# Cross attention and FFN, two layers: the product with V in two pairs of groups instead of four single groups

## What is computed

```python
# block 1: attention with a band, then a crossing of neighbouring sequences
scores = einsum(q, k) / sqrt(8)            # 8 heads of 8 channels
scores = where(abs(i - j) <= 64, scores, lowest)
o = softmax(scores) @ v                    # then out projection, relu, * ctx, w_ct
# block 2: out = x @ weight * scale, scaled down by its norm (tanh and clip)
# block 3: attention over all positions, q and k rotated, k and v from ctx
# block 4: x @ dequantised w_up + LoRA, relu, @ dequantised w_down + LoRA
```

## Time and profile before

| | us |
|---|---|
| median of 3 runs | 1336.01 (1335.77 to 1337.31) |
| profiled execution, its own time | 1332.8 |
| its span | 1331.0 |
| PE busy, share of the span | 1259.3, 95% |
| DVE busy | 906.8, 68% |
| ACT busy | 848.2, 64% |
| POOL busy | 676.3, 51% |

### The profile page before, as it was taken

How to read it: one execution, slowest core, us unless ns; L and a number is a source line. 1 busy time by engine, 2 the same in 40 slices (tenths; PEclk the granted TensorE clock), 3 DMA queues, 4 the chain that set the end, 5 groups by cost and what they waited for, 6 DMA issues and landing times.

```text
span 1331.0 us, 35488 instructions
## 1 busy us (share of the span) xinstructions
PE 1259.3 (95%) x11100; PEld 836.7 (63%) x11100; DVE 906.8 (68%) x1924; ACT 848.2 (64%) x1849; POOL 676.3 (51%) x1169
## 2 busy tenths in 40 slices
PE   6999999999999998768899999999999989999998
PEld 3667676767766765544565656666666546666665
DVE  6878878887888873659999988888888842111110
ACT  2566777767777775556888888888888853222111
POOL 4577788787878765055455445555555211000000
PEclk9999999999999998988999999999999999999999
DMA  8554555445544430033444444444454400000000
GB/s 208 121 135 106 117 119 117 103 117 116 116 113 112 102 85 6 13 80 89 93 105 94 96 95 103 112 103 101 103 113 99 85 2 16 16 16 16 16 16 32
DMA packets 90486, 113.34 MB, mean 85 GB/s; under 512 B 13971, under 2 KB 80275, under 8 KB 82739
## 3 DMA queue, kind: packets, MB, share of 16 engines
q1 hardware_dynamic: 89216, 111.25, 36.3%
q10 hardware_dynamic: 1206, 1.29, 0.3%
HBM read 18.66 MB, written 4.19 MB: 17 GB/s over the span
## 4 chain that ended last, share of the span: by engine, by line
PE 72%; DVE 9%; POOL 6%; issue 4%; ACT 3%; DMA 3%; SPq 1%; POOLq 0%; ACTq 0%; DVEq 0%
PE bank L477 13%; PE bank L437 12%; PE bank L453 11%; PE bank L699 8%; PE bank L690 8%; PE bank L435 5%; DVE row_max L1131 5%; POOL probs L1355 4%; PE bank L489 4%; PE bank L541 2%; PE bank L508 2%; DMA Ks<-Ks 1%; PE bank L648 1%; PE bank L518 1%; PE bank L529 1%
## 5 line engine op out<-in xcount | busy, mean ns | idle before, releaser
L1131 DVE TENSOR_REDUCE row_max<-bank 128x2 f32<-128x384 f32 (+1 forms) x1024 | 597.7, 616 | 110.5 <-PE bank L437 106.2
L735 ACT ACTIVATE probs<-bank 128x384 f32<-128x384 f32 (+1 forms) x1024 | 536.8, 542 | 162.2 <-PE bank L453 151.5
L437 PE MATMUL bank<-Ks,Qs 96*128 96x192 bf16 (+1 forms) x2048 | 372.1, 263 | 15.1 <-DVE row_max L1131 8.8
L453 PE MATMUL bank<-Qs,Ks 128*128 128x192 bf16 (+1 forms) x2048 | 365.6, 260 | 13.5 <-ACT probs L735 12.4
L1355 POOL TENSOR_SCALAR_AFFINE_SELECT probs<-probs 128x256 f32<-128x256 f32 (+1 forms) x512 | 259.3, 530 | 98.7 <-ACT probs L735 78.3
L437 PEld LDWEIGHTS bank<-Ks,Qs 96*128 96x128 bf16 x2048 | 186.7, 99 | 125.8 <-DVE row_max L1131 39.4
L477 PE MATMUL bank<-probs,V 128*32 128x192 f32 (+1 forms) x4096 | 248.3, 360 | 7.2 <-POOL probs L1355 5.9
L453 PEld LDWEIGHTS bank<-Qs,Ks 128*128 128x128 bf16 x2048 | 185.7, 97 | 45.4 <-ACT probs L735 31.7
L435 PE MATMUL bank<-band,ident 128*128 128x384 bf16 x512 | 168.6, 329 | 1.4 <-DMA Ks<-Ks 1.0
L477 PEld LDWEIGHTS bank<-probs,V 128*32 128x32 f32 x4096 | 107.3, 109 | 87.2 <-issue 43.8
L1292 DVE TENSOR_TENSOR X<-bank,X 128x256 f32 (+1 forms) x32 | 13.6, 424 | 185.6 <-PE bank L699 185.6
(11 more groups left out here) (114 smaller groups left out, 1614.3 us busy)
## 6 DMA issues: line engine op xcount, KB each, us to landing
Ks<-Ks SPq DMA_DIRECT2D x64, 576.0 KB
Qs<-Qs SPq DMA_DIRECT2D x128, 192.0 KB
Qs<-Qp SPq DMA_DIRECT2D x192, 64.0 KB
Ks<-Kp SPq DMA_DIRECT2D x192, 64.0 KB
X<-in_x SPq DMA_DIRECT2D x4, 1024.0 KB, 13.4
side<-in_ctx_crossed SPq DMA_DIRECT2D x32, 128.0 KB, 2.1
side<-in_ctx SPq DMA_DIRECT2D x32, 128.0 KB, 2.1
out<-X SPq DMA_DIRECT2D x8, 512.0 KB, 3.0
```

What stands on the lines that cost most here:

```text
L437: last = nc.tensor.matmul(dst[:, blk * win:(blk + 1) * win], Qs[0:SHIFT_ROW, pair[1], h, blk * P:(blk + 1) * P], Ks[0:SHIFT_ROW, pair[1], ...
L453: last = nc.tensor.matmul(dst[:, blk * win:(blk + 1) * win], Ks[:, pair[1], h, blk * P:(blk + 1) * P], Qs[:, pair[1], h, start(blk):start( ...
L735: nc.scalar.activation(probs[:, h % 8, 0:2 * win], exp_bank[h % 2][:, 0:2 * win], ACT.Exp, scale=SCALE).then_inc(s["exped"], 1)
L1131: nc.vector.tensor_reduce(row_max[:, pair[1], h // HEADS, 0, h % HEADS * 2:h % HEADS * 2 + 2], bank_of(pair, h)[:, 0:2 * win].rearrange("p ...
```

## The change

The groups of the product with V are issued two at a time: at head 3 groups 2 and 3 of the pair before, at head 11 groups 0 and 1 of the pair (heads 2 and 10 in layer 1). `probs` gets 12 slots instead of 8, `q_rest` and `k_rest` get one buffer each instead of three, and their writers wait for the split of the pair before. The tiles of the middle stage move to slots 8 to 11 and to `heads_sb`, with one more wait on ACT and an earlier one on DVE.

```diff
--- before.py
+++ after.py
@@ -24,6 +24,7 @@
 OUTSIDE = -1.0e30
 WIN = T // 2 + BAND
 RING = 3
+PROBS = 12
 FFN_BLOCKS = 8
 VALUES_AT = (3, 2)
 X_CHUNKS = 4
@@ -124,14 +125,14 @@
 
         Qs = sb("Qs", [P, RING, HPP, T], bf16)
         Ks = sb("Ks", [P, RING, HPP, T], bf16)
-        probs = sb("probs", [P, 8, 2 * T])
+        probs = sb("probs", [P, PROBS, 2 * T])
         V = sb("V", [P, RING, 2 * 4 * V_STEP])
         xn = sb("xn", [P, RING, T])
         side = sb("side", [P, RING, T])
         Qp = sb("Qp", [P, RING, PARTS, T], bf16)
         Kp = sb("Kp", [P, RING, PARTS, T], bf16)
-        q_rest = sb("q_rest", [P, RING, T])
-        k_rest = sb("k_rest", [P, RING, T])
+        q_rest = sb("q_rest", [P, T])
+        k_rest = sb("k_rest", [P, T])
         rot = sb("rot", [P, 4, T])
         row_max = sb("row_max", [P, RING, 2, PARTS, HPP])
         max_rows = sb("max_rows", [PARTS * HPP, 2, P], bf16)
@@ -145,9 +146,9 @@
 
         ff = sb("ff", [P, PAIRS, T])
 
-        ff0_xT = [probs[:, n // 2, n % 2 * T:(n % 2 + 1) * T] for n in range(FF0_RING)]
-        ff0_xn = [probs[:, 2 + n // 2, n % 2 * T:(n % 2 + 1) * T] for n in range(FF0_RING)]
-        junk = probs[:, 4, :].rearrange("p (a t) -> p a t", a=2)
+        ff0_xT = [probs[:, PROBS - 4 + n // 2, n % 2 * T:(n % 2 + 1) * T] for n in range(FF0_RING)]
+        ff0_xn = [probs[:, PROBS - 2 + n // 2, n % 2 * T:(n % 2 + 1) * T] for n in range(FF0_RING)]
+        junk = heads_sb[:, :].rearrange("p (a t) -> p a t", a=2)
         xT = (Ks[:, 0:2, :, :].rearrange("p a h t -> p (a h t)").bitcast(fp32)[:, 0:4 * T * 2]
               .rearrange("p (a b t) -> p a b t", a=2, b=2))
         ffn_raw = ff[:, 0:PAIRS // 2, :].rearrange("p (n k) t -> p n (k t)", k=2).bitcast(i32)
@@ -156,7 +157,7 @@
         lora_in = lora[:, 0:T + FF]
         lora_out = lora[:, T + FF:2 * (T + FF)]
         hidden = [Qs[:, 0:2, :, :].rearrange("p a h t -> p (a h t)").bitcast(fp32)
-                  .rearrange("p (h t) -> p h t", h=FF // P), probs]
+                  .rearrange("p (h t) -> p h t", h=FF // P), probs[:, 0:FF // P, :]]
 
         bank = [stack.enter_context(nc.psum_tensor(f"bank{n}", [P, 512], fp32)) for n in range(8)]
         exp_bank, pv_bank = bank[2:4], bank[4]
@@ -238,6 +239,10 @@
 
             return part.bitcast(bf16)[:, 1::2]
 
+        def slot_of(pair, h):
+
+            return (HPP * pair[1] + h) % PROBS
+
         def bank_of(pair, h):
 
             return score_bank[(HPP * pair[1] + h) % SCORE_BANKS]
@@ -476,10 +481,15 @@
                         column = (blk * 4 + g) * V_STEP + 32 * j - (g % 2) * (HD + 1)
                         last = nc.tensor.matmul(dst[32 * j:32 * j + 32, first:first + win],
                                                 V[:, pair[1], column:column + 32],
-                                                probs[:, head % 8, blk * win:(blk + 1) * win],
+                                                probs[:, slot_of(pair, head), blk * win:(blk + 1) * win],
                                                 start=(g % 2 == 0 and blk == 0), stop=(g % 2 == 1 and blk == 1),
                                                 skip_group_check=True)
                 last.then_inc(s["pv_done"], 1)
+
+            def values_half(pair, half):
+
+                for g in (2 * half, 2 * half + 1):
+                    values_group(pair, g)
 
             def project(b, name, pair, weight, source, wait):
                 if not active(pair):
@@ -553,7 +563,7 @@
                                                normed[:, pair[1], blk, :, :].rearrange("p a c -> p (a c)"), ident[:, :])
                 last.then_inc(s["B_filled"], 1)
 
-            tail = {0: lambda: values_group(TAIL, 3), 2: lambda: turn_heads(TAIL), 4: lambda: turn_back(TAIL),
+            tail = {0: lambda: values_half(TAIL, 1), 2: lambda: turn_heads(TAIL), 4: lambda: turn_back(TAIL),
                     5: lambda: project_out(TAIL)}
             if l == 0:
                 tail[6] = lambda: cross_mix(at(TAIL, -1))
@@ -585,8 +595,8 @@
                         turn_max("A", p1, 0)
                     score_head(p1, h)
                     shifted_head(r, h)
-                    if h % 4 == VALUES_AT[l]:
-                        values_group(m1 if h < 4 else r, (h // 4 - 1) % 4)
+                    if h % HEADS == VALUES_AT[l]:
+                        values_half(m1 if h < HEADS else r, 1 - h // HEADS)
 
             def run(first):
                 iterations(e, iteration, extra and (lambda n: extra(e, n)), last=False, first=first)
@@ -731,8 +741,8 @@
                 n = num(pair) * HPP + h
                 e.wait_ge(s["shifted"], n + 1)
                 if h % 4 == 0:
-                    wait_some(e, s["pv_done"], num(pair) * 4 + h // 4 - 1)
-                nc.scalar.activation(probs[:, h % 8, 0:2 * win], exp_bank[h % 2][:, 0:2 * win], ACT.Exp,
+                    wait_some(e, s["pv_done"], num(pair) * 4 + h // 4 - PROBS // 4 + 1)
+                nc.scalar.activation(probs[:, slot_of(pair, h), 0:2 * win], exp_bank[h % 2][:, 0:2 * win], ACT.Exp,
                                      scale=SCALE).then_inc(s["exped"], 1)
 
             def high_part(bk, name, pair, parts, column):
@@ -749,7 +759,7 @@
                 else:
                     e.wait_ge(s["rot_sum"], num(pair) * 2 + (1 if name == "q" else 2))
                     rest = q_rest if name == "q" else k_rest
-                    nc.scalar.activation(parts[:, u, 0, :], rest[:, u, :],
+                    nc.scalar.activation(parts[:, u, 0, :], rest[:, :],
                                          ACT.Copy).then_inc(s[f"{name}_high"], 1)
 
             def turn_rows(bk, name, pair, n, column):
@@ -936,6 +946,8 @@
             def between(n):
                 if n in tail:
                     tail[n]()
+                if n == FF0_LAG[1]:
+                    wait_job(e, L[0], 0, "A", "heads", TAIL, "filled")
                 if n == 8:
                     root(0, 0, FIRST_CHUNK)
                 if n == 10:
@@ -1137,8 +1149,8 @@
                 if not active(pair):
                     return
                 e.wait_ge(s[f"{name}_high"], num(pair) + 1)
-                wait_some(e, s[f"{name}_parts"], num(pair) - RING + 1)
-                nc.vector.scalar_tensor_tensor(out=rest[:, pair[1], :], in0=job_bank[bk][:, 0:T],
+                wait_some(e, s[f"{name}_parts"], num(pair))
+                nc.vector.scalar_tensor_tensor(out=rest[:, :], in0=job_bank[bk][:, 0:T],
                                                scalar=b[:, column:column + 1], in1=parts[:, pair[1], 0, :],
                                                op0=ALU.add, op1=ALU.subtract).then_inc(s[f"{bk}_read"], 1)
 
@@ -1274,7 +1286,7 @@
                     iteration(*early(-2)[:1])
 
             e.wait_ge(ffn_ready, PREP_BLOCKS)
-            e.wait_ge(L[0]["pv_done"], PAIRS * 4 - 1)
+            e.wait_ge(L[0]["pv_done"], PAIRS * 4 - 2)
             ff0_steps(ff0, between)
             e.wait_ge(f_keep, PAIRS)
             run(-1, loop_from=4)
@@ -1319,14 +1331,14 @@
                 else:
 
                     e.wait_ge(s[f"{name}_high"], num(pair) + 1)
-                    nc.gpsimd.tensor_tensor(rest[:, u, :], rest[:, u, :], parts[:, u, 0, :],
+                    nc.gpsimd.tensor_tensor(rest[:, :], rest[:, :], parts[:, u, 0, :],
                                             ALU.subtract).then_inc(s[mid], 1)
                     wait_apart(e, (s[mid], num(pair) * 2 + 1))
                     n, total = num(pair), 2
-                nc.gpsimd.tensor_scalar(parts[:, u, 1, :], rest[:, u, :], 1.0, None,
+                nc.gpsimd.tensor_scalar(parts[:, u, 1, :], rest[:, :], 1.0, None,
                                         ALU.mult).then_inc(s[mid], 1)
                 e.wait_ge(s[mid], (n + 1) * total)
-                nc.gpsimd.tensor_tensor(parts[:, u, 2, :], rest[:, u, :], parts[:, u, 1, :],
+                nc.gpsimd.tensor_tensor(parts[:, u, 2, :], rest[:, :], parts[:, u, 1, :],
                                         ALU.subtract).then_inc(s[done], 1)
 
             def rot_sum(bk, name, pair, n, rest):
@@ -1338,8 +1350,8 @@
                                         ALU.mult).then_inc(s["rot_mul"], 1)
                 wait_job(e, s, l, bk, name, pair, "read")
                 e.wait_ge(s["rot_mul"], num(pair) * 2 + n + 1)
-                wait_some(e, s[f"{name}_parts"], num(pair) - RING + 1)
-                nc.gpsimd.tensor_tensor(rest[:, pair[1], :], rot[:, 2 * n, :], rot[:, 2 * n + 1, :],
+                wait_some(e, s[f"{name}_parts"], num(pair))
+                nc.gpsimd.tensor_tensor(rest[:, :], rot[:, 2 * n, :], rot[:, 2 * n + 1, :],
                                         ALU.add).then_inc(s["rot_sum"], 1)
 
             def mask_group(pair, g):
@@ -1347,7 +1359,7 @@
                 if not active(pair):
                     return
                 wait_apart(e, (s["exped"], num(pair) * HPP + 4 * g + 4))
-                first = (g % 2) * 4
```

(1 more changed line is left out.)

## The result

| | before | after |
|---|---|---|
| median | 1335.89 us (1335.19 to 1337.31, 4 runs) | 1360.71 us (1359.1 to 1362.4, 4 runs) |
| profiled execution | 1332.8, span 1331.0 | 1361.61, span 1359.8 |
| granted clock, whole span | 0.984 | 0.981 |
| an iteration of layer 0 (pairs 5 to 25) | 15.00 us | 14.96 us |
| an iteration of layer 1 (pairs 11 to 25) | 14.68 us | 15.93 us |

A forecast was written before the change was run, and what follows sets the result against it. TensorE's queue was taken to bound the kernel. Layer 0's -2 us and layer 1's +16.4, +0.7 and +0.7 gave +16: profiled 1332.8 to 1349, median 1352 (chance 0.72), range 1337 to 1367.

The forecast's parts named there:

- Savings: TensorE's entries and groups cheaper in pairs, late mask in layer 0 gone: 0.65 us an iteration in layer 0, 0.48 in layer 1.
- rival (a): All savings come through in both layers, with no new waits: 33 us, 1303; chance 0.05.
- First, the landing: Next pair's shifted head 0 waits for the maxima's transfer: 0.83 us in layer 1, 0.40 in layer 0 (net 0.26).
- Rival (c): At head 0 the maxima's transfer lands 0.24 us sooner, in 2.03: waits 0.59 and 0.16, total 1340; chance 0.05.
- Second, ACT at head 7: Layer 1: shifted head 7 waits 0.52 us for ACT's exponential of head 5; bounds nothing and 0.96.
- Third, DVE's maxima at head 9: Scores of head 9 wait for DVE's maximum of head 6: 0.25 us in layer 0, 0.13 in layer 1.
- Fourth, SP at head 8 in layer 0: One iteration in three, shifted head 8 waits 0.48 us for late-sent maxima, replacing head 9's 0.25; mean 0.33.
- (b): ACT and DVE keep up at heads 7 and 9, only the maxima's landing costs: 1330, faster; chance 0.07.
- (e): TensorE, waiting more, falls more often to its lower clock of 1.2 GHz, costing some 15 us: 1367; chance 0.07.

The follow-up runs named there:

- single_first1: Changed kernel, but layer 1 with groups 2 and 3 together at head 2, group 0 alone at head 6, group 1 alone at head 10: 1343.33 us.
- slots_only: Changed kernel with its 12 slots, single rests and moved tiles, but the four groups one by one at their old heads in both layers: 1336.76 us.
- maxima_early0: Changed kernel, but in layer 0 the next pair's maxima are transposed and copied at head 11, the transpose ahead of the burst: 1415.24 us.
- single_last1: Changed kernel, but layer 1 with group 3 of the pair before at head 2, groups 0 and 1 at head 10, group 2 at head 14: 1353.41 us.
- bank_b_three: Changed kernel; groups 0, 1 at head 12 (layer 1: group 0 at 6), maxima turned in bank B (layer 0), split before q's rest (layer 1): 1326.40 us.

## Why the prediction came out as it did

The sign and the mechanism were right, the size was short by 9 us (16 to 25), inside the range.

**Savings (right).** 0.65 and 0.48 forecast; -0.65 and -0.47 measured. The bursts take 1.44 in layer 0 and 1.86 to 1.87 in layer 1, as worked out, and the late mask at head 15 no longer holds a group. The Trainium skill's rule (TensorEngine Tiling (Array Packing), Key Properties) that a change of the tiling mode drains TensorE agrees with the entries of 0.09 that went; taken alone it gave rival (a), 1303, and the rows of waits have the answer to that.

**First, the landing (right).** Issue to landing is 2.21 to 2.28 in layer 0 (pairs 5 to 25) and 2.27 to 2.32 in layer 1 (pairs 11 to 25), and the matmul starts 0.05 later, or 0.12 in one iteration of three. 0.76 for 0.83 in layer 1, 0.44 for 0.40 in layer 0. Rival (c) needed 2.03, from the Trainium skill's sum (DMA: Bandwidth & Descriptors, Anatomy of one DMA), and falls; the one landing in the trace of before was the better guide. That 0.14 would come back at the transpose of head 3 was too much: 0.07 did.

**Second, ACT at head 7 (right, a size off).** 0.64 for 0.52. ACT kept to my times: from the end of the burst at head 2 (869.53) to its exponential of head 5 (872.53) it is 3.00, forecast 2.99. TensorE was early: it could have started shifted head 7 at 872.34 + 0.22, 3.03 and not 3.12 after the burst, because the projection and the turned heads at head 5 took 0.87 and not 0.95, as they no longer wait.

**Third, DVE's maxima at head 9 (wrong).** The waits of 0.25 in layer 0 and of 0.13 in layer 1 do not exist. In layer 0 DVE's normalisation became up to 0.26 shorter, which is as much as the wait was to be; in layer 1 the waits at heads 7 and 8, 0.9 together, stand ahead of it (that these two are the causes is my reading, no run tests it).

**Fourth, SP at head 8 in layer 0 (mis-sized).** 0.07 on average for the 0.33 of steps three and four. In the one iteration of three the transfer did land last, after 2.96 on average for the estimated 3.1, but the path from SP's issue to shifted head 8 shrank from 3.53 only to 2.86 without the wait, by 0.67 and not 0.9: a wait of 0.22 for the forecast 0.48. Why the path shrank less was not found. With step three in it, layer 0 has 0.26 less than forecast; against that stand 0.11 more in the first step and 0.17 of small ones that I had not counted. So layer 0's -0.04 for a forecast of -0.06 is partly luck.

**The term that was missing.** In layer 1 the turning back at head 8 waits 0.26 for DVE to read bank B, and its transposes take 0.05 more. I had asked who reads each result that TensorE waits for, and not who still reads each bank that it writes. The rows were there: the group at head 6 stood between k's turned rows and L552 as it stood before shifted head 7. single_first1, which puts one group there, removes this wait and the one at head 7 at once. 0.31 of the missing 0.33 per iteration is this term. The 0.11 more at heads 14 and 15 are cancelled by the 0.13 at head 9 that did not come.

**The sum.** Layer 1: 16 iterations at +1.25 are 20; seven early ones cost 0.3 each and not 0.1 (15.50 to 15.81 over pairs 3 to 8), 2 us; the iteration of pair 10 took 17.3 before and 19.1 after, 1.8; the rest of the 25.3 is what the first three and the last four iterations add, 0.7 and 0.8. The 1.8 of pair 10 is not the pairing's: the iteration takes 18.9 in slots_only too, whose plan is that of before. The granted clock in it was 1.00 before and 0.91 in both the others, and 19.1 x 0.09 is 1.7. In the iteration of pair 30 it is the other way round: it was longer before (19.2 us, granted clock 0.82) than after (17.7).

**The other rivals.** (b) needed the waits at heads 7 and 9 under 0.2 to 0.3: layer 0 fulfils it, layer 1 does not at head 7 (0.64). Its -0.39 for layer 0 did not come either, since the landing and the small waits took it. (e) falls as the cause of the 25 us: the granted clock of the last stretch stays at 0.99, with 7.8% of it idle. A part of it shows elsewhere: the whole span was granted 0.981 for 0.984, which is 4 us of the 28.8 between the two profiled spans, most of them behind layer 1; and maxima_early0 with 1.81 us more of idle time per iteration ran layer 0 at 0.97.

## What to carry to other kernels

A piece of work that fills an engine's queue is also a delay that others rely on, for the readers of the banks it stands in front of as well as for its own inputs. Before moving it, list for the first instruction behind it every input and every earlier reader of its output, with the time each has to spare, and move the piece only past those with more to spare than it is long. Here two groups of 1.10 us each stood in front of work with 0.31 us and less to spare, and moving either cost more than the 0.24 that pairing it saved. Pairing paid in layer 0 alone, and only once the inputs of the next step had been made early.

## What was not expected of the hardware

- DVE's `TENSOR_SCALAR` of 128x256 took 0.40 us with POOL idle, and 0.51 to 0.66 where a POOL instruction beside it ended 0.36 to 0.52 us after its start; one that ended 0.13 to 0.22 us after its start cost nothing.
- At the turn of the loop of three iterations the changed kernel's TensorE loses 0.3 to 0.4 us between shifted head 15 and the next scores: 0.64 instead of 0.23 in layer 1, 0.50 to 0.55 instead of 0.17 in layer 0. Before the change the same turn cost nothing (0.22 in layer 1 each time), nor does it in layer 1 of single_last1, which has a group at head 14. It looks like one more thing that those groups covered; no run tests it apart. In the changed kernel most of it comes out of the wait for the landing (0.61 at shifted head 0 instead of 0.94); in bank_b_three it stays, over 0.1 of an iteration in each layer.
- The transposes of the turning back took 0.27 from start to start behind a wait (layer 1 of the changed kernel) and right behind a group (layer 0 before), and 0.22 in the other two cases.
